# Moving an output bias from two GpSimd instructions a batch into TensorE's accumulation

## The reference

```
qkv = h @ W_qkv.T + b_qkv              # h: (8, 512, 256), layer norm * (1 + ca) + sa
attn = softmax(q k^T per head and block of 64)
x = x + ga * ((attn @ v) @ W_out.T + b_out)   # ga: (8, 1, 256)
```

## Time and profile before

| | |
|---|---|
| median of 3 runs | 1993.46 us (1992.79 to 1993.63) |
| the profiled execution | 1993.63 us |
| its span, first to last instruction | 1992.1 us |
| TensorE busy | 1937.0 us, 97% |
| VectorE busy | 1126.0 us, 57% |
| ScalarE busy | 936.0 us, 47% |
| GpSimd busy | 720.2 us, 36% |
| mean granted clock of TensorE | 0.990 |

### The profile page before, as it was taken

The page is one execution under the profiler, slowest core; times in us unless marked ns, Lnnn a source line. Parts: engine busy times, 40 slices in busy tenths (PEclk is TensorE's granted clock), DMA queues, the critical chain, the costliest instruction groups (busy, mean ns, idle before and its releaser), DMA issues.

```text
span 1992.1 us, 30474 instructions
## 1 busy us (share of the span) xinstructions
PE 1937.0 (97%) x11192; PEld 1317.2 (66%) x11192; DVE 1126.0 (57%) x2904; ACT 936.0 (47%) x2040; POOL 720.2 (36%) x835
## 2 busy tenths in 40 slices
PE   7988999999999999999999999999999999999998
PEld 5734655665566566556655655555677788888887
DVE  6875566557565856665585667467543447322321
ACT  3744565566556555655665665444443421111111
POOL 4302334333434333343334333244343433333332
PEclk9987999999999999999999999999999999999999
DMA  3021001000100100010001000040112133333333
GB/s 126 1 75 35 1 1 38 12 12 1 38 22 1 35 5 22 1 39 12 12 1 38 22 1 26 22 162 1 38 22 72 20 93 74 78 82 77 80 77 69
DMA packets 59697, 76.78 MB, mean 39 GB/s; under 512 B 7120, under 2 KB 52824, under 8 KB 59296
## 3 DMA queue, kind: packets, MB, share of 16 engines
q1 hardware_dynamic: 46448, 57.28, 8.8%
q0 software_dynamic: 12288, 16.79, 5.0%
q10 hardware_dynamic: 816, 0.79, 0.1%
HBM read 53.71 MB, written 21.00 MB: 37 GB/s over the span
## 4 chain that ended last, share of the span: by engine, by line
PE 89%; DVE 6%; ACT 2%; DMA 1%; issue 1%; POOL 0%; SPq 0%; DVEq 0%; POOLq 0%; ACTq 0%
PE bank L738 12%; PE bank L951 11%; PE bank L964 11%; PE bank L801 6%; PE bank L825 4%; PE bank L837 4%; PE bank L856 4%; PE bank L752 3%; PE bank L564 3%; PE bank L723 3%; PE bank L869 3%; PE bank L590 3%; PE bank L810 3%; PE bank L788 2%; PE bank L685 2%; PE bank L616 1%
## 5 line engine op out<-in xcount | busy, mean ns | idle before, releaser
L951 PE MATMUL bank<-xin,ew 128*128 128x256 f32 x1024 | 235.6, 382 | 0.0
L1191 ACT ACTIVATE h<-bank 128x512 f32<-128x512 f32 x128 | 76.0, 597 | 326.0 <-PE bank L951 325.9
L964 PE MATMUL bank<-ew,h 128*128 128x256 f32 x1024 | 227.5, 379 | 0.0
L964 PEld LDWEIGHTS bank<-ew,h 128*128 128x128 f32 x1024 | 194.0, 190 | 27.5 <-issue 1.3
L951 PEld LDWEIGHTS bank<-xin,ew 128*128 128x128 f32 x1024 | 189.2, 190 | 26.4 <-issue 2.7
L1771 POOL DMA_INDIRECT out<-y,indices x64 | 102.8, 1607 | 284.4 <-DVE y L1627 196.9
L1733 POOL TENSOR_TENSOR s<-s,ri 128x256 f32<-128x256 f32 (+3 forms) x128 | 161.2, 1275 | 120.6 <-DVE ri L1490 120.6
L1167 ACT ACTIVATE s<-s,mn 128x128 f32<-128x128 f32 (+3 forms) x256 | 141.0, 552 | 119.4 <-DVE mn L1483 119.2
L1468 DVE SCALAR_TENSOR_TENSOR th<-th,bank 128x384 f32<-128x384 f32 (+1 forms) x192 | 106.2, 595 | 124.0 <-ACT th L1158 123.7
L1627 DVE SCALAR_TENSOR_TENSOR y<-bank,gates,gbe 128x256 f32<-128x256 f32 x64 | 30.8, 483 | 247.3 <-PE bank L964 247.2
L1716 POOL TENSOR_SCALAR_AFFINE_SELECT th<-th 128x256 f32<-128x256 f32 (+1 forms) x96 | 46.8, 488 | 309.7 <-DVE th L1468 309.6
(11 more groups left out here) (318 smaller groups left out, 3688.9 us busy)
## 6 DMA issues: line engine op xcount, KB each, us to landing
ew<-L_ffn_w SPq DMA_DIRECT2D x24, 1024.0 KB, 8.5
x1s<-x_scratch SPq DMA_DIRECT2D x8, 512.0 KB, 4.8
out<-x1s SPq DMA_DIRECT2D x8, 512.0 KB, 2.9
xn_scratch<-n_xn SPq DMA_DIRECT2D x8, 512.0 KB, 2.9
x<-L_attn_x SPq DMA_DIRECT2D x7, 512.0 KB, 3.8
x_scratch<-x SPq DMA_DIRECT2D x7, 512.0 KB, 3.2
wqkv<-w_qkv SPq DMA_DIRECT2D x1, 3072.0 KB, 9.9
wqkv<-L_wmod SPq DMA_DIRECT2D x2, 1024.0 KB, 7.7
```

Source lines behind the costliest of these rows:

```text
L951: mm = te.matmul(banks[i][:, g * 2 * P:(g + 1) * 2 * P], w1[:, kk, (2 * n + g) * P:(2 * n + g + 1) * P], xin[:, kk, :, :].rearrange("p h s ...
L964: mm = te.matmul(banks[i][:, 0:D], ex.h1[:, g, n * P:(n + 1) * P], w2[:, g, :], start=(g == 0), stop=(g == FC - 1))
```

## The change

`bias0` goes, on GpSimd and in all three places of the order. The row is added in PSUM instead: in `out0` each token tile gets one more matmul at the end of its accumulation, with a stationary operand of ones (3 rows, 128 columns, bf16) and `bout_parts` (3 rows, 256 columns, bf16) as the moving one. The three rows are the bias split in three bf16 parts whose sum carries fp32's precision. `setup0` makes them: `bout` is now loaded into 3 rows, the v bias is spread over 3 columns, and eight VectorE instructions in a row split it. Row 0 keeps the first part, row 1 the second and row 2 the remainder, picked with columns of the identity matrix. VectorE's `out0` now waits for the gate row's load. GpSimd fills the ones at the start.

```diff
@@ the order: 0bias0:0, 1bias0:0 of HEAD and +bias0:0 of PERIOD are taken out @@
@@ TensorE @@
-                mm = te.matmul(banks[i][:, 0:D], f.a1[:, kk, 0:P], b0.wout[:, kk, :], start=(kk == 0),
+                mm = te.matmul(banks[i][0:3, 0:D], b0.bv3[:, kk, :], b0.wout[:, kk, :], start=(kk == 0),
                                stop=(kk == KC - 1))
...
                 for kk in range(KC):
-                    mm = te.matmul(out, f.aT[:, kk, t * P:(t + 1) * P], b0.wout[:, kk, :], start=(kk == 0),
-                                   stop=(kk == KC - 1))
+                    te.matmul(out, f.aT[:, kk, t * P:(t + 1) * P], b0.wout[:, kk, :], start=(kk == 0), stop=False)
+                mm = te.matmul(out, c_.ones[:, :], b0.bout_parts[:, :], start=False, stop=True)
             mm.then_inc(full[i], 1)
@@ VectorE @@
-N_SETUP = 7 + KC
+N_SETUP = 17 + KC
...
-            v.tensor_copy(f.a1[:, :, 0:P], b0.bv[:, :].unsqueeze(2).to_broadcast([P, KC, P])).then_inc(s["bv_ready"], 1)
+            v.tensor_copy(b0.bv3[:, :, :], b0.bv[:, :].unsqueeze(2).to_broadcast([P, KC, 3])).then_inc(s["bv_ready"], 1)
...
+            bout, parts = b0.bout[:, :], b0.bout_parts[:, :]
             i, nth = at[step, b, n, 0]
             v.wait_ge(full[i], nth)
-            v.tensor_tensor(b0.bout[:, :], b0.bout[:, :], banks[i][:, 0:D], ALU.add).then_inc(drained[i], 1)
+            v.tensor_tensor(bout, bout, banks[i][0:3, 0:D], ALU.add).then_inc(drained[i], 1)
+            v.wait_ge(drained[i], nth)
+            kept = [f.a2[0:3, h * D:(h + 1) * D] for h in range(2)]
+            n_setup = 7 + KC
+            for h in range(2):
+                v.tensor_copy(parts, bout).then_inc(done, 1)
+                v.wait_ge(done, n_setup + 1)
+                v.tensor_scalar(kept[h], parts, c_.ident[0:3, h:h + 1], None, ALU.mult).then_inc(done, 1)
+                v.tensor_tensor(bout, bout, parts, ALU.subtract).then_inc(done, 1)
+                v.wait_ge(done, n_setup + 3)
+                n_setup += 3
+            v.scalar_tensor_tensor(out=bout, in0=bout, scalar=c_.ident[0:3, 2:3], in1=kept[0], op0=ALU.mult,
+                                   op1=ALU.add).then_inc(done, 1)
+            v.wait_ge(done, n_setup + 1)
+            v.tensor_tensor(parts, bout, kept[1], ALU.add).then_inc(done, 3)
             v.wait_ge(done, N_SETUP)
...
         elif step == "out0":
             if n == 0:
-                v.wait_ge(f.sem["x0_bias"], 2 * (lap + 1))
+                v.wait_ge(f.sem["ga0_in"], 16 * (lap + 1))
@@ GpSimd @@
+    g.memset(c_.ones[:, :], 1.0).then_inc(done, 1)
...
-        elif step == "bias0":
-            gated = f.a2[:, 0:D]
...
-            g.wait_ge(f.sem["ga0_in"], 16 * (lap + 1))
-            g.wait_ge(f.sem["xn"], (3 * lap + 1) * NT)
-            g.tensor_tensor(gated, f.ga[:, :], b0.bout[:, :], ALU.mult).then_inc(f.sem["x0_bias"], 1)
-            g.wait_ge(f.sem["x0_bias"], 2 * lap + 1)
-            g.tensor_tensor(f.x[:, :, :], f.x[:, :, :], gated.unsqueeze(1).to_broadcast([P, NT, D]), ALU.add
-                            ).then_inc(f.sem["x0_bias"], 1)
@@ SP @@
-            sp.dma_start(b0.bout[:, :], d["L0_attn_b_out"].partition_broadcast(P)).then_inc(done, 16)
+            sp.dma_start(b0.bout[:, :], d["L0_attn_b_out"].partition_broadcast(3)).then_inc(done, 16)
```

More of the change, by code:

```diff
@@ L54 @@
     0w0_load:0 0rows:0 0feat:0 0kq:0 1norm:0 1mod_load:0 0kq:1 1mod_load:1 1feat:0 0setup0:0 0sc0:0 0sc0:1
[L55 to L63, removed]
+    0ga0_load:0 0wt0:0 1silu:0 1kq:0 0wt0:1 1kq:1 0sc0:2 0v:0 0sc0:3 0tp0:0 0tp0:1 1sc0:0 1ga0_load:0 0wt0:2 0wt0:3
@@ new lines @@
+    0v:1 1wt0:0 1v:0 1sc0:1 0sc0:4 1wt0:1 0tp0:2 0pv0:0 1tp0:0 0wt0:4 0tp0:3 1sc0:2 1sc0:3 1tp0:1 1wt0:2 1wt0:3 1v:1
+    0pv0:1 0sc0:5 1sc0:4 1tp0:2 0wt0:5 1tp0:3 1pv0:0 1wt0:4 0tp0:4 0sc0:6 0sc0:7 0wt0:6 0wt0:7 0tp0:5 1pv0:1 1tp0:4
+    1sc0:5 1cols:0 0w1_load:0 0tp0:6 0pv0:2 1wt0:5 0tp0:7 1sc0:6 1tp0:5 1wt0:6 0pv0:3 1sc0:7 1pv0:2 1wt0:7 0out0:0
+    0out0:1 1tp0:6 0stats:1 0norm:1 1tp0:7 1pv0:3 1out0:0 0feat:1 1out0:1 1stats:1 0cn1:0 0gc:0 0cn2:0 0twist:0
+    1norm:1 0gc:1 0cn3:0 0gc:2 0cn4:0 1feat:1 0cn1:1 1cols:1 0cn2:1 1cn1:0 1rows:0 0tables:0 0cn3:1 1gc:0 0cn4:1
@@ L64 @@
+    1cn2:0 1gc:1 1twist:0 1cn3:0 1gc:2 1cn4:0 0cn1:2 1cn1:1 0cn2:2 1cn2:1 1cn3:1 0cn3:2 1cn4:1 0cn4:2 1cn1:2 1cn2:2
+    0gate0:0 1cn3:2 1cn4:2 1gate0:0 0fin0:0 1fin0:0 0stats:2 1stats:2 0norm:2 1norm:2 0feat:2 1feat:2
 """
 PERIOD = """
-    -x1_load:0 proj:0.0 +x0:0 +stats:0 proj:0.1 +norm:0 proj:0.3 +ga0_load:0 +bias0:0 proj:0.2 proj:0.4 -weigh:11
-    +feat:0 look:0.0 term:0 look:0.1 look:0.2 -attend:10 -turn:11 +kq:0 +kq:1 turn_vu:0 -attend:11 vc:0 +sc0:0
-    +wt0:0 +sc0:1 look:0.3 +sc0:2 vc:1 +tp0:0 w:0.0 +v:0 +v:1 +wt0:1 +wt0:2 +tp0:1 +sc0:3 -o_out:3 +tp0:2 +wt0:3
@@ L72 @@
[L72 to L81, removed]
@@ L82 @@
-    su:10 sw:10 attend:8 o_out:2 weigh:9 w:3.1 +feat:2 sc:10 weigh:10 su:11 turn:9 sw:11 sc:11 attend:9 turn:10
+    -x1_load:0 proj:0.0 +x0:0 +stats:0 proj:0.1 +norm:0 proj:0.3 +ga0_load:0 proj:0.2 proj:0.4 -weigh:11 +feat:0
+    look:0.0 term:0 look:0.1 look:0.2 -attend:10 -turn:11 +kq:0 +kq:1 turn_vu:0 -attend:11 vc:0 +sc0:0 +wt0:0 +sc0:1
+    look:0.3 +sc0:2 vc:1 +tp0:0 w:0.0 +v:0 +v:1 +wt0:1 +wt0:2 +tp0:1 +sc0:3 -o_out:3 +tp0:2 +wt0:3 proj:1.2 +sc0:4
+    +pv0:0 +sc0:5 -out1:0 +wt0:4 +wt0:5 +tp0:3 -out1:1 su:0 proj:1.0 -stats_t:0 sw:0 sc:0 +sc0:6 vc:2 +tp0:4 +tp0:5
@@ new lines @@
+    +wt0:6 +pv0:1 w:0.1 proj:1.1 +sc0:7 vc:3 turn_vu:1 weigh:0 su:1 sw:1 sc:1 +pv0:2 +wt0:7 +tp0:6 weigh:1 proj:1.4
+    turn:0 proj:1.3 -norm_t:0 +tp0:7 su:2 sw:2 look:1.0 look:1.1 +pv0:3 look:1.2 sc:2 term:1 look:1.3 w:1.0 attend:0
+    turn:1 weigh:2 +out0:0 +out0:1 +stats:1 proj:2.1 proj:2.3 su:3 +norm:1 attend:1 sw:3 -feat_t:0 turn:2 +feat:1
+    su:4 proj:2.0 sw:4 sc:3 sc:4 attend:2 +cn1:0 o_out:0 +twist:0 weigh:3 +gc:0 turn:3 -gate:0 +cn2:0 weigh:4
+    proj:2.2 -softmax:0 +gc:1 +cn3:0 w:1.1 +gc:2 +cn4:0 look:2.0 look:2.1 look:2.2 proj:2.4 turn_vu:2 su:5 +cn1:1
@@ new lines @@
+    look:2.3 sw:5 +cn2:1 attend:3 +cn3:1 turn:4 sc:5 term:2 weigh:5 +cn4:1 proj:3.3 +cn1:2 proj:3.2 w:2.0 attend:4
+    su:6 +cn2:2 turn:5 sw:6 -probs:0 +cn3:2 attend:5 o_out:1 sc:6 weigh:6 su:7 w:2.1 sw:7 +cn4:2 proj:3.0 proj:3.1
+    sc:7 look:3.0 turn:6 su:8 +gate0:0 sw:8 look:3.1 turn_vu:3 weigh:7 +fin0:0 look:3.2 sc:8 term:3 look:3.3 weigh:8
+    attend:6 w:3.0 turn:7 +stats:2 proj:3.4 su:9 sw:9 attend:7 turn:8 sc:9 +norm:2 su:10 sw:10 attend:8 o_out:2
+    weigh:9 w:3.1 +feat:2 sc:10 weigh:10 su:11 turn:9 sw:11 sc:11 attend:9 turn:10
@@ L284, in __init__ @@
         self.sign = sb("sign", [P, 1])
+        self.ones = sb("ones", [3, P], BF16)
         self.power = sb("power", [P, NT])
@@ L308, in __init__ @@
         self.bv = sb("bv", [P, KC])
-        self.bout = sb("bout", [P, D])
+        self.bout = sb("bout", [3, D])
+        self.bout_parts = sb("bout_parts", [3, D], BF16)
         self.w1 = sb("cw1", [P, KC, D])
@@ L327, in __init__ @@
         self.sar = sb("sar", [P, 3])
+        self.bv3 = sb("bv3", [P, KC, 3])
         self.turned = sb("cw1t", [P, D])
@@ L434 @@
 FIRST_SEMAPHORES = [
-    "x0_in", "ga0_in", "x1_out", "stats", "mv", "rstd", "xn", "x0_bias", "mx0", "exp0", "all0", "ri0", "weighted0", "x0_mid",
+    "x0_in", "ga0_in", "x1_out", "stats", "mv", "rstd", "xn", "mx0", "exp0", "all0", "ri0", "weighted0", "x0_mid",
     "gf_base", "cycle", "activated", "combined", "h_next", "h_gated",
@@ L489, in off @@
     return P * j * (j + 1) // 2
-N_POOL_CONST = 12
+N_POOL_CONST = 13
 COLS = ((0, 2 * KC), (2 * KC, NMOD))
@@ L1310, in vector_engine @@
             v.memset(b0.sar[:, 2:3], 0.1).then_inc(done, 1)
+            bout, parts = b0.bout[:, :], b0.bout_parts[:, :]
             i, nth = at[step, b, n, 0]
             v.wait_ge(full[i], nth)
-            v.tensor_tensor(b0.bout[:, :], b0.bout[:, :], banks[i][:, 0:D], ALU.add).then_inc(drained[i], 1)
+            v.tensor_tensor(bout, bout, banks[i][0:3, 0:D], ALU.add).then_inc(drained[i], 1)
[13 more added lines that the diff above has]
+            v.tensor_tensor(parts, bout, kept[1], ALU.add).then_inc(done, 3)
+            assert n_setup + 4 == N_SETUP
             v.wait_ge(done, N_SETUP)
@@ L1668, in pool_engine @@
                 g.memset(state.k[:, :, :, :, :], 0.0).then_inc(s["setup_pool"], 1)
-        elif step == "bias0":
-            gated = f.a2[:, 0:D]
-            if b < 2:
-                i, nth = at["setup0", 0, 0, 0]
-                g.wait_ge(drained[i], nth)
-            g.wait_ge(f.sem["ga0_in"], 16 * (lap + 1))
-            g.wait_ge(f.sem["xn"], (3 * lap + 1) * NT)
-            g.tensor_tensor(gated, f.ga[:, :], b0.bout[:, :], ALU.mult).then_inc(f.sem["x0_bias"], 1)
-            g.wait_ge(f.sem["x0_bias"], 2 * lap + 1)
-            g.tensor_tensor(f.x[:, :, :], f.x[:, :, :], gated.unsqueeze(1).to_broadcast([P, NT, D]), ALU.add
-                            ).then_inc(f.sem["x0_bias"], 1)
         elif step == "wt0":
```

## The result

The changed kernel takes 2005.91 us (median; 2005.73 to 2008.22) against 1993.55 us: 12.4 us slower by the medians, ratio 1.0063, 95% interval 1.0046 to 1.0081. I had forecast 1996.8 us and no difference that can be told, in a range that ended at 2000.3.

A forecast was written before the change was run, and what follows sets the result against it. TensorE, running without a gap, was taken to bound the kernel; 32 added matmuls at 0.108 us, +3.46, less 0.12 gained in the head, made +3.3 us, 1996.8 us for the median, range 1993.7 to 2000.3 us.

The forecast's parts named there:

- What bounds the kernel: TensorE runs without a gap at out0: an added instruction is paid in full, GpSimd's 24.6 us removed gain nothing.
- the price of the added matmul: On TensorE in out0, each of 32 added bf16 matmuls costs 0.108 us, 3.46 us in all, following weight load hidden.
- the bound from above: An added bf16 matmul in out0 costs at most one fp32 instruction of the same columns, 0.216 us, 6.9 us in all.
- the sign of being wrong: In steady out0, the forecast is wrong if the four bf16 instructions take 0.8 us or more.
- The three prices that I used: TensorE prices from the trace before: fp32 instruction of 256 columns 0.216 us, bf16 matmul of 5 columns 0.034, fp32 load 0.106.
- The rival of dearer matmuls: In out0, each bf16 instruction or its load is not hidden: 0.216 us apiece, 6.9 us, 2000.2 us; chance 0.24.
- setup0: In the head, eight more VectorE instructions take 2.80 us, making VectorE 2.32 us late; cost to the kernel nothing.
- the wait I named: VectorE's 2.25 us wait for a transpose ahead of 49.39 us in the head, by which the 2.32 us delay is gone.
- term of 0.12 us gained: In the head, TensorE's 1.00 us wait for the copy of bv shrinks by 0 to 0.28 us, taken as 0.12.
- The low clock: Rival: in the first two batches' cycles, low-clock stretches more or less shift the time, 1993.0 to 2000.6 us; chance 0.11.

## Why the prediction was wrong

- **What bounds the kernel** held: added work on TensorE was paid in full in every lap, and taking 24.6 us from GpSimd gave nothing (no bias step, 0.9996).
- **The step that failed is the price of the added matmul.** I took 0.108 us and set 0.216 as the bound from above; it is 0.408. The columns were sized right (0.108, shown with 128 and 96 rows). What was missing is 0.30 us for each passage to a 3-row matmul and back. The four of a batch cost 1.63 us, beyond the 0.8 that I had named as the sign of being wrong. The sentence "A weight load of 0.106 us fits just under 0.108, so the fp32 load that follows stays hidden" is what fell: the load does fit (with 128 rows it lies there), but beside a matmul of 3 rows it is not laid there.
- **The bound was built on the wrong neighbour.** The three prices that I used are all of matmuls of 128 rows. I searched by columns and type, and the form differed most in rows. I wrote that a matmul of 3 rows between ones of 128 is in no row, and let the bound stand.
- **The trace of before had signs of it,** in rows that the prediction does not use. The chain above has the price of a change of columns. And there are the same eight transposes of the same line, once ahead of a group of 128 rows and once ahead of one of 64 (timeline of TensorE, before):

```profile
91.68 1.04 PE L549 MATMUL bank<-ident,n_xn 128*128 128x128 f32 x8
92.55 1.89 PE L632 MATMUL bank<-wout,a1b 128*128 128x256 f32 x8
```

```profile
347.73 1.04 PE L549 MATMUL bank<-ident,n_xn 128*128 128x128 f32 x8
348.69 0.49 PE L752 MATMUL bank<-qu,ku 64*128 64x128 f32 x4
```

From start to start 0.87 us in the first case and 0.96 in the second: 0.09 us more ahead of 64 rows, about what the entry costs here (0.21 less 0.11). That this is the same thing is argued from the likeness; I did not test it at that place.

- **The rival of dearer matmuls** had the sign, the place and half of the mechanism (loads that are not hidden), at 0.216 us and 2000.2 us, with 0.24. By the rule that I cited beside it (the Trainium skill, TensorE: Matmul & The Clock Gate, "The mechanism") loads are hidden only where row groups differ (the same section also lets a load into a background weight buffer run ahead, which I left out). The runs agree that such loads can be exposed, and disagree on where: loads that share all 128 or 96 rows with the matmul in flight are hidden, and it is the 3, 32 and 64-row ones beside them that are not.
- **setup0** was right: 2.8 us forecast, 3.1 found, delay gone at the wait I named, and no loss in the kernel without the added matmul (0.9995). Its term of 0.12 us gained was not: TensorE's wait for the copy of bv did shrink, from 1.00 to 0.87 us, but the eight fp32 instructions behind the setup matmul, whose stationary operand now has 3 columns, take 1.92 us in place of 1.73.
- **The low clock** did move by a stretch in the profiled run; the 12.4 us between the medians are explained without it.
- **Range and chances:** slower had 0.35, and the range ended 5.6 us short. The bound alone accounts for that: 32 x (0.408 - 0.216) = 6.1 us.

Not shown: why the passage costs 0.1 us going in and 0.2 coming out (the two loads in the open have 0.20 of the 0.30), why a change of columns costs 0.15, and what makes the 0.09 us between two fp32 instructions of 3 rows. Not tried: a regrouping of the kernel's own steps of 64 rows or 64 columns.

## What to carry to other kernels

On a TensorE that runs without gaps, price an added matmul by the shape of its neighbours' stationary operands as well as by its moving columns: look in the trace for weight loads that start together with their matmul. If a small constant must be added among matmuls of 128 rows, give its operands 96 or 128 rows, filled with zeros (0.11 us in place of 0.41 here), or put the small ones side by side so that they share a passage. And before moving work off an engine, delete it once: the kernel without its bias step showed a ceiling of 0.14% here for whatever takes its place.

## What the runs showed of the hardware

- A passage from fp32 matmuls of 128 rows to a bf16 one of 3, 32 or 64 rows and back costs 0.30 us beside the columns, 0.10 before it and 0.20 behind; with an fp32 one of 3 rows it is the same, and 0.09 more between its two instructions. From 128 to 96 rows and back it costs nothing.
- Between stationary operands of 64 and 128 columns, all of 128 rows, each change costs 0.15 us (0.81 against 0.66).
- A bf16 matmul of 256 columns among fp32 ones costs 0.11 us when it has 96 or 128 rows, and the four fp32 instructions behind it keep their 0.86 to 0.87: the change of type costs nothing.
- The load of the 3-row operand takes 0.09 us, that of 128 rows in bf16 0.10: leaving rows out saves 0.01 us on the load.
